# A third way to get turned tokens: from the third batch on they are loaded turned, GpSimd normalizes them there, and ScalarE scales the last expert

## The reference, cut to what matters

```python
x = L0_attn_x                                   # (8, 512, 128)
xn = (x - mean(x)) / sqrt(var(x) + 1e-5)        # over the 128 features
q, k, v = xn @ Wq.T, xn @ Wk.T, xn @ Wv.T
s = softmax((q @ k.T) * tril(ones) / sqrt(512)) # masked scores are 0, not -inf
gates = softmax(xn @ Wg); keep the top 2 of 8, scaled to sum 1
ffn = sum_e gate[:, e] * (xn @ We[e] + be[e])
out = x + s @ v + ffn
```

## Time and profile before

| | us |
|---|---|
| median of 3 runs | 120.28 (120.26 to 120.3) |
| profiled execution | 120.22 |
| its span | 118.5 |
| TensorE busy | 112.7 (95%) |
| VectorE busy | 106.4 (90%) |
| ScalarE busy | 99.0 (84%) |
| GpSimd busy | 91.3 (77%) |

### The profile page before, as it was taken

One profiled execution on the slowest core, in us unless ns is written; L12 is line 12 of the kernel. 1 busy time (PEld: TensorE's weight loads), 2 busy tenths in 40 slices (PEclk: granted clock), 3 DMA queues, 4 the chain that ended last, 5 costly groups with the idle time before them and its releaser, 6 DMA issues.

```text
span 118.5 us, 2933 instructions
## 1 busy us (share of the span) xinstructions
PE 112.7 (95%) x733; PEld 103.5 (87%) x733; DVE 106.4 (90%) x532; ACT 99.0 (84%) x338; POOL 91.3 (77%) x183
## 2 busy tenths in 40 slices
PE   4986999999999999999999999999999999999990
PEld 4965879998999989998899989999899989899990
DVE  0689999989999899999999899999999898998892
ACT  2456899899897999899997989899997989978930
POOL 7349569899768996699768995799868995896970
PEclk9999999999999999999999999999999999999999
DMA  3759500000300011000300020000300030000033
GB/s 95 255 165 304 157 3 6 0 3 3 89 0 3 0 55 39 0 0 3 94 3 0 0 68 20 6 0 3 94 0 0 0 90 4 0 3 0 6 91 89
DMA packets 9233, 5.18 MB, mean 44 GB/s; under 512 B 384, under 2 KB 9088, under 8 KB 9216
## 3 DMA queue, kind: packets, MB, share of 16 engines
q1 hardware_dynamic: 8656, 4.66, 13.6%
q10 hardware_dynamic: 560, 0.33, 1.0%
HBM read 2.89 MB, written 2.10 MB: 42 GB/s over the span
## 4 chain that ended last, share of the span: by engine, by line
PE 87%; DMA 4%; ACT 3%; DVE 2%; SPq 1%; issue 1%; DVEq 0%
PE ring L248 15%; PE ring L252 14%; PE ring L249 14%; PE attb L306 13%; PE score L293 8%; PE score L252 4%; PE score L249 4%; PE score L248 4%; DMA w_f<-in_w_stacked_dram 4%; PE ring L324 3%; PE ring L345 2%; PE attb L358 1%; PE ring L335 1%; PE ring L337 1%; PE ring L334 1%; ACT c_s L906 1%
## 5 line engine op out<-in xcount | busy, mean ns | idle before, releaser
L922 ACT ACTIVATE ysc<-ring,gate 128x128 f32<-128x128 f32 x124 | 35.6, 388 | 0.8 <-PE ring L252 0.6
L248 PE MATMUL ring<-w_hi,xT_hi 128*128 128x512 f32 (+2 forms) x96 | 35.5, 370 | 0.4 <-ACT xT_hi L1001 0.4
L249 PE MATMUL ring<-w_lo,xT_hi 128*128 128x512 f32 (+2 forms) x96 | 32.5, 339 | 0.0
L252 PE MATMUL ring<-w_hi,xT_lo 128*128 128x512 f32 (+2 forms) x96 | 32.5, 338 | 0.0
L1130 POOL TENSOR_TENSOR ysc<-ysc,mix 128x256 f32<-128x256 f32 x31 | 22.9, 738 | 6.2 <-DVE mix L576 3.6
L1127 POOL TENSOR_TENSOR ysc<-ysc 128x256 f32<-128x256 f32 x31 | 22.8, 736 | 6.0 <-ACT ysc L922 6.0
L576 DVE SCALAR_TENSOR_TENSOR mix<-ring,gate,mix 128x128 f32<-128x128 f32 x65 | 22.4, 347 | 0.9 <-PE ring L252 0.3
L306 PE MATMUL attb<-c_s,probT 128*128 128x128 f32 x152 | 21.8, 274 | 0.0
L306 PEld LDWEIGHTS attb<-c_s,probT 128*128 128x128 f32 x152 | 20.1, 191 | 0.2
L248 PEld LDWEIGHTS ring<-w_hi,xT_hi 128*128 128x128 f32 x96 | 18.1, 189 | 2.1 <-ACT xT_hi L1001 0.6
L252 PEld LDWEIGHTS ring<-w_hi,xT_lo 128*128 128x128 f32 x96 | 18.1, 188 | 1.5 <-DVE xT_lo L509 0.2
(11 more groups left out here) (115 smaller groups left out, 237.8 us busy)
## 6 DMA issues: line engine op xcount, KB each, us to landing
x_all<-in_x_dram SPq DMA_DIRECT2D x7, 256.0 KB, 3.9
out_dram<-o_s SPq DMA_DIRECT2D x7, 256.0 KB, 2.3
w_f<-in_w_stacked_dram SPq DMA_DIRECT2D x1, 256.0 KB, 4.5
w_f<-in_w_stacked_dram SPq DMA_DIRECT2D x1, 192.0 KB, 4.4
w_f<-in_w_stacked_dram SPq DMA_DIRECT2D x1, 132.0 KB, 3.7
x_all<-in_x_dram ACTq DMA_DIRECT2D x1, 128.0 KB, 2.7
x_all<-in_x_dram SPq DMA_DIRECT2D x1, 128.0 KB, 2.5
wqk_s<-in_w_attention_dram ACTq DMA_DIRECT2D x1, 128.0 KB, 3.9
```

The costliest lines, as they stand in the source:

```text
L248: nc.tensor.matmul(dst, hi, w_h, start=True, stop=False)
L249: nc.tensor.matmul(dst, hi, w_l, start=False, stop=False)
L252: return nc.tensor.matmul(dst, lo, w_h, start=False, stop=True)
L922: last = nc.scalar.mul(ysc[:, t, e, :], bank(f"A{t}", b)[:, e * P:(e + 1) * P], gate[:, b % 2, t, e:e + 1])
```

## The change

- The host hands over a second copy of x with each batch turned (`x_turned`). SP loads it for batches 2 to 7, six loads of 256 KB behind the loads of x.
- For these batches nothing is normalized on ScalarE or turned on TensorE. The rstd and mean of each token (`norm`, 4 + 4 numbers on each partition) are written to DRAM and read back to all 128 partitions (`spread_norms`), and GpSimd subtracts and multiplies whole 128 x 512 tiles (`normalize_turned`). `x_hi`, `x_lo` and `token_sums` read the result `xnT` in SBUF instead of the PSUM bank X.
- Statistics are taken one batch earlier: iteration n handles batch n+2 in place of n+1.
- The eighth expert is scaled by ScalarE in every batch, tile by tile; `mix` gets five slots, so that this may be written while the batch before is still read.
- The orders of TensorE, VectorE, ScalarE and GpSimd and the three lists of ring groups are written anew.

```diff
-GROUPS = "B2- C3 A3- B3- SV DT- B0 A0 X+ A1 B1 U+ C0+ C1+ A2 C2+".split()
+GROUPS = "B2- C3 A3- A0 B3- SV DT- B0 A1 C0+ C1+ C2+ B1 U+ A2".split()
+MIX_AT = (0, 1, 3)
...
+            for b in range(2, B):
+                sp.dma_start(xt_all[:, b - 2, :], x_turned[b]).then_inc(S["xt_rest"], 16)
+            def spread_norms(b):
+                if b >= B:
+                    return
+                sp.wait_ge(S["rstd_ready"], b + 1)
+                sp.wait_ge(S["nmean_ready"], b + 1)
+                sp.dma_start(norms[b].rearrange("c (t p) -> p c t", p=P), norm[:, b, :, :], allow_slow_non_contiguous=True
+                             ).then_inc(S["norm_out"], 16)
+                sp.wait_ge(S["norm_out"], 16 * (b - 1))
+                if b >= 4:
+                    sp.wait_ge(S["xnT_ready"], b - 3)
+                sp.dma_start(norm_rows[:, b % 2, :, :].rearrange("p c n -> p (c n)"),
+                             norms[b:b + 1].rearrange("b c n -> b (c n)").to_broadcast([P, 2 * NT * P])).then_inc(S["norm_in"], 16)
...
+            spread_norms(2)
             for b in range(B - 1):
+                spread_norms(b + 3)
                 store(b)
...
     (TensorE, one iteration)
-                transpose_x(n + 1)
                 wide(n, "A", 1)
+                scores(n, 3)
+                transpose_probs(n, 1)
+                wide(n + 1, "C", 0)
+                wide(n + 1, "C", 1)
+                wide(n + 1, "C", 2)
                 wide(n, "B", 1)
...
     (VectorE: normal_finish)
-                nc.vector.tensor_scalar(nmean[:], mv[:, :, 0], -1.0, None, ALU.mult).then_inc(S["nmean_ready"], 1)
+                if b < 2:
+                    nc.vector.tensor_scalar(nmean[:], mv[:, :, 0], -1.0, None, ALU.mult).then_inc(S["nmean_ready"], 1)
+                else:
+                    nc.vector.tensor_copy(norm[:, b, 1, :], mv[:, :, 0]).then_inc(S["nmean_ready"], 1)
...
     (VectorE: x_lo; x_hi and token_sums take their source in the same way)
-                split_lo(xT_lo[:, b % 2, :], bank("X", b)[:], xT_hi[:, b % 2, :], S["xl_ready"])
+                source = xnT[:, b % 2, :] if b > 1 else bank("X", b)[:]
+                split_lo(xT_lo[:, b % 2, :], source, xT_hi[:, b % 2, :], S["xl_ready"])
...
     (VectorE, one iteration, its second half)
+                gate_out(n)
+                softmax_rec(n - 1)
                 mix_b(n - 1, 3, 0)
+                negate_max(n, 0)
+                mask_scores(n, 1)
+                normal_finish(n + 2)
...
                 mix_b(n, 0, 0)
+                finish_tile(n - 1, 0)
                 sv_rows(n, 2)
                 mix_b(n, 0, 1)
+                x_lo(n + 1)
                 mix_b(n, 0, 2)
+                token_sums(n + 1)
...
     (ScalarE: scale_last_act, now called in every batch)
-                act.wait_ge(S["ffn_ready"], b * NT)
-                for t in range(NT - 1):
-                    last = nc.scalar.mul(mix[:, t, 3, :], c_s[:, b % 2, t, Y_AT:Y_AT + P], gate[:, b % 2, t, 7:8])
+                if b > 1:
+                    act.wait_ge(S["ffn_ready"], (b - 1) * NT)
+                for t in range(NT if b < B - 1 else NT - 1):
+                    last = nc.scalar.mul(mix[:, t, 2 + 2 * (b % 2), :], c_s[:, b % 2, t, Y_AT:Y_AT + P], gate[:, b % 2, t, 7:8])
...
     (GpSimd; normal_rstd(b) is one pow for b != 1, written to norm)
+            def normalize_turned(b):
+                pool.wait_ge(S["xt_rest"], 16 * (B - 2))
+                pool.wait_ge(S["norm_in"], 16 * (b - 1))
+                if b >= 4:
+                    pool.wait_ge(S["xl_ready"], b - 1)
+                    pool.wait_ge(S["xsum_ready"], b - 1)
+                y = xnT[:, b % 2, :]
+                chain.step(nc.gpsimd.tensor_tensor(y, xt_all[:, b - 2, :], norm_rows[:, b % 2, 1, :], ALU.subtract))
+                nc.gpsimd.tensor_tensor(y, y, norm_rows[:, b % 2, 0, :], ALU.mult).then_inc(S["xnT_ready"], 1)
...
             for n in range(1, B - 1):
-                normal_rstd(n + 1)
+                normalize_turned(n + 1)
+                normal_rstd(n + 2)
                 sum_experts(n - 1, 3)
-                scale_last(n)
                 sum_experts(n, 0)
                 sum_experts(n, 1)
                 sum_experts(n, 2)
                 bias_rows(n)
```

More of the change, by code:

```diff
@@ L79, in step, with build @@
         self.need(self.mark(instruction))
-def build(nc, x, w_attention, w_stacked, be_rows, out):
+def build(nc, x, w_attention, w_stacked, be_rows, x_turned, norms, out):
     B, T, D = x.shape
@@ L416, in _ @@
             wide(1, "C", 2)
+            project_u(1)
+            wide(0, "A", 2)
+            transpose_probs(0, 1)
             for n in range(1, B - 1):
@@ L748, in _ @@
             normal_stats(1, 3)
+            token_sums_pairs(0)
             normal_finish(1)
@@ L765, in _ @@
+            normal_stats(2, 2)
+            gate_sum(0)
+            normal_stats(2, 3)
+            gate_rec(0)
+            sv_rows(0, 2)
+            gate_out(0)
+            normal_finish(2)
+            x_lo(1)
+            negate_max(0, 1)
             mix_b(0, 0, 0)
+            token_sums(1)
             mix_b(0, 0, 1)
             mix_b(0, 0, 2)
-            x_lo(1)
-            token_sums(1)
             for n in range(1, B - 1):
+                mask_scores(n - 1, 2)
                 mix_b(n - 1, 1, 0)
-                mask_scores(n - 1, 2)
+                negate_max(n - 1, 2)
@@ L843, in _ @@
             gate_sum(B - 1)
             gate_rec(B - 1)
+            mix_b(B - 2, 3, 1)
+            gate_out(B - 1)
+            mix_b(B - 2, 3, 2)
+            mix_b(B - 1, 0, 0)
+            mask_scores(B - 1, 1)
+            mask_scores(B - 1, 2)
+            mix_b(B - 1, 0, 1)
             negate_max(B - 1, 1)
-            gate_out(B - 1)
-            mask_scores(B - 1, 2)
-            mix_b(B - 1, 0, 0)
+            mix_b(B - 1, 0, 2)
             negate_max(B - 1, 2)
             mask_scores(B - 1, 3)
-            mix_b(B - 1, 0, 1)
+            token_sums_later(B - 1)
@@ L967, in x_hi @@
                     act.wait_ge(S["scores_done"], (b - 1) * NT)
-                nc.scalar.copy(xT_hi[:, b % 2, :], bank("X", b)[:]).then_inc(S["xh_ready"], 1)
+                source = xnT[:, b % 2, :] if b > 1 else bank("X", b)[:]
+                nc.scalar.copy(xT_hi[:, b % 2, :], source).then_inc(S["xh_ready"], 1)
             def sv_high(b):
@@ L1129, in sum_experts @@
                 pool.wait_ge(S["mix_ready"], b * NT + t + 1)
-                chain.step(nc.gpsimd.tensor_tensor(y[:, 0:2, :], y[:, 0:2, :], mix[:, t, 2:4, :], ALU.add))
+                chain.step(nc.gpsimd.tensor_tensor(y[:, 0:2, :], y[:, 0:2, :], mix[:, t, 2 + b % 2:4 + b % 2, :], ALU.add))
                 if b > 1:
@@ L1218, in _ @@
             bias_rhs_blocks(0)
-            scale_last(0)
+            normal_rstd(2)
             sum_experts(0, 0)
```

269 lines of the change are left out of this document (127 added, 142 removed).

## The result

The changed kernel takes 159.75 us (159.2 to 160.08, four runs) against 120.27 us (120.2 to 120.3): a ratio of 1.328, 95% interval 1.324 to 1.332. The forecast was 122.3 us with a range to 125.5. It is far outside.

What follows compares the result with a forecast made beforehand. TensorE bounded the kernel at 13.24 us; VectorE and GpSimd sharing a port would make periods 13.6. Iterations 1 to 5 +1.8, iteration 6 -0.44, start +0.7: +2.1 on 120.22 gives 122.3 us; 8-of-10 range 117.8 to 125.5.

Steps and rivals of the forecast that it cites:

- The way of the norms: Norms from SBUF to DRAM and back to all partitions: write 3.5 us, read back 3.2 to 4.8, costed at nothing.
- the trip: Writing the norms out and reading them back with issues: 7.5 to 9.1 us, hidden within a period less 3.6 us.
- The rival of the late norms: Write of 5.4 us or more makes normalize_turned wait, periods grow, 1 to 2 us in six batches; 126 us, chance 0.13.
- Its rule on transfers below 512 bytes: Norms' write: engines read, modify and write below 512 B; at twice 30 ns per write, the trip is 1.9 us longer.
- start: Before the steady periods: first norms' trip and batch 2's statistics delay things by 0 to 2 us, taken as 0.7.
- the last part: Iteration 6, which has neither pow nor statistics: a gain of 0.44 us.
- GpSimd and ScalarE by their clocks: Work per period: GpSimd 12.87 us with two added operations at 1.28 each, ScalarE 11.9 us, below TensorE's 12.80.
- The shared port: VectorE's x_lo with two SBUF sources and GpSimd lock each other out: GpSimd loses 0.60 us, x_lo waits 0.37.
- caught once as feared: Short VectorE instructions such as normal_finish, beside normalize_turned, wait for GpSimd; one per batch at 0.64 us makes VectorE's period 14.00.
- TensorE's loss of 2.64 us: Token turns leave TensorE in batches 2 to 7, 6 x 0.44 us; its period falls from 13.24 to 12.80 us.

Runs made afterwards that it cites:

- e7: Kernel before the change plus test writes to DRAM: 1024 single numbers took 9.9 us, 128 single numbers 8.1, 128 pieces of 32 bytes 2.1.
- e11: Kernel before the change plus test writes of 128 pieces: single numbers side by side 8.1 us, 64 or 512 bytes apart 2.1, 32-byte pieces 2.7.
- e1: Changed kernel, each partition writing its eight norms as one 32-byte piece, GpSimd reading them with a step of eight: 123.9 us, ratio 1.031.
- e4: Changed kernel without the norms' write and its wait, the read back kept but taking numbers of x (wrong result): 122.84 us, ratio 1.022.
- e5: Kernel without the norms' write and its wait, with x_lo reading a PSUM bank of wrong contents instead of xnT: 121.06 us, ratio 1.009.
- e6: Changed kernel, norms in two writes of 128 16-byte pieces, turned x loaded in (partition, tile) order, GpSimd writing back in token order: 123.26 us, ratio 1.026.

## Why the prediction was wrong, step by step

- **The way of the norms: wrong, and this step decided.** "Writing out is 1024 single numbers ... 64 per DMA engine are 1.9 us on top of the 1.6 us": 3.5 us were 9.5 to 12.2. I priced a write by the mean time of a packet in a queue full of large ones. e7 shows that the count is hardly the price, e11 that lying side by side is, e1 that with pieces of 32 bytes 35.8 us go. So the sum had the trip at nothing (7.5 to 9.1 us, hidden), where it took 15 to 17 us. Reading back was 4.1 to 4.6 us in five batches and 5.4 in one (taken 3.2 to 4.8).
- **The rival of the late norms: right mechanism, wrong size.** It had 0.13 and 126 us. Its rule holds: the trip may take the period less 3.6 us, and each period grows by the excess. That is the same as the circle, period = trip + 3.6 us: 15.6 + 3.6 = 19.2 (measured 19.4 in the window above). What it lacked was the write's size again: it began at a write of 5.4 us and priced the excess at 1 to 2 us a batch, where 15.6 - (13.13 - 3.6) is 6.1. Five periods from the first read back (27.39) to the last (125.88) took 98.5 us against 5 x 13.13 = 65.7 in e4: 32.8 us. The first norms came 6.9 us late (`normalize_turned` at 32.91 against 26.04). Together 39.7, of which the spans (158.4 and 119.7) show 38.7. The upper end of the range, 125.5 us, left out even most of this rival.
- **The Trainium skill, DMA: Bandwidth & Descriptors, section "Specifications".** Its rule on transfers below 512 bytes I had weighed as 1.9 us. The runs do not bear it out as a matter of size alone: 32-byte pieces (2.1 to 2.7 us) were no slower than 512-byte ones (2.6), nor were single numbers that lay 64 bytes apart (2.1).
- **All the rest: 122.3 forecast, 122.84 in e4, but by other terms.** Period 13.13 in place of 13.6 (-2.3 us over five), start +2.1 to +2.8 in place of +0.7, the last part -1.0 in place of -0.44, and 1.1 us outside the span that no term stood for. That the two sums agree is luck.
- **GpSimd and ScalarE by their clocks: right.** `normalize_turned` is 1.27 and 1.29 us (taken 1.28), ScalarE's work of a period 11.84 (taken 11.9), GpSimd's 12.80 without the hold, steps between instructions included (taken 12.87). VectorE was busy 12.97 us and waited for nothing (taken 12.99 to 14.0, as the longest); the 13.6 that the sum took for the period rested on it.
- **The shared port: the mechanism right, its price too high.** `x_lo` is 0.68 to 0.97 us, median 0.84: 0.16 more, not 0.37. GpSimd loses 0.33 to 0.46 us in one instruction of every batch, not 0.60, and 12.80 + 0.33 is the period; I had made VectorE the longer of the two. `normal_finish` was caught once as feared: its copy took 1.25 us beside GpSimd's `normalize_turned`. e5 gives the sum: 1.6 us for the kernel, of which 5 x 0.18 = 0.9 in the periods; where the rest lies I did not trace. By the Trainium skill, SBUF — State Buffer, section "SBUF: two separate sides", whichever of the two starts first keeps the other out for its whole instruction; the traces now agree for GpSimd as the loser too (1.18 us in place of 0.74).
- **TensorE's loss of 2.64 us: never collected.** The floor of 12.80 was not reached by any version, 12.95 in e5 being the nearest, with TensorE busy throughout: there the turns' going brought 0.29 us a period, not 0.44. At the period of e4 the gain is 5 x 0.11 = 0.6 us, and the start takes more than that.

## What to carry to other kernels

Here a small transfer was priced by how its pieces lay at the target, not by its bytes or the mean packet. Before numbers are scattered to DRAM, let each partition write one piece, and measure that write alone; with a wrong price even a right rule for the rival says nothing. When an engine's queue holds both the end of a trip and the start of the next one, the period is the trip plus what stands between; walk the circle once before calling a transfer hidden. And where the sum hits but its terms do not, as here without the trip, the agreement is luck: compare the windows term by term.

## What the runs showed of the hardware

- 128 numbers of 4 bytes written to DRAM took 8.1 us side by side and 2.1 us when 64 or 512 bytes apart; pieces of 8 and 16 bytes side by side took 3.3 and 3.2 (e11, each once).
- GpSimd's 128 x 512 product took 1.65 us reading one source with a step of 32 bytes (e1) and 1.30 us writing its result with a step (e6), against 1.26 in the changed kernel.
- A GpSimd sum that met VectorE's `x_lo` with two sources in SBUF took 1.06 to 1.20 us in place of 0.74 (e4); with one source of `x_lo` in PSUM it stayed at 0.74 (e5).
